# Leaving out the 18 products of zeros with which TensorE begins

## The reference

```
# layer 0: an FFN with low-rank corrections chosen by batch, then 4 rounds of a mixture of experts
h   = relu(x @ wi.T + 2*(x @ ca.T) @ cb.T + 2*(x @ Ea[id].T) @ Eb[id].T)
y   = h @ wo.T + 2*(...common...) + 2*(...expert id of the batch...)
for r in range(4):
    top2 softmax weights cw from y @ Wg[r] + bg[r]          # 4 experts
    y += sum_e cw[e] * (gelu(y @ W1[e] + b1[e]) @ W2[e] + b2[e])
x = x + y
# layer 1: a low-rank map chosen by batch, then a gated FFN
z = (x @ A[lang].T) @ B[lang].T + emb[lang]
g = silu(z @ w1.T * s1) * (z @ w2.T * s2)
g = gelu(g @ h1.T * t1);  g = gelu(g @ h2.T * t2);  x = x + g @ w3.T * s3
```

## Time and profile before

| | us |
|---|---|
| median of 3 runs | 488.02 (486.09 to 488.29) |
| profiled execution | 487.44 |
| its span, first to last instruction | 485.4 |
| TensorE busy | 479.3 (99% of the span) |
| ScalarE, VectorE busy | 393.9, 386.7 |
| GpSimd busy | 119.0 |

### The profile page before, as it was taken

The page is one execution under the profiler, slowest core; times in us unless marked ns, Lnnn a source line. Parts: engine busy times, 40 slices in busy tenths (PEclk is TensorE's granted clock), DMA queues, the critical chain, the costliest instruction groups (busy, mean ns, idle before and its releaser), DMA issues.

```text
span 485.4 us, 7484 instructions
## 1 busy us (share of the span) xinstructions
PE 479.3 (99%) x2276; PEld 397.8 (82%) x2276; DVE 386.7 (80%) x640; ACT 393.9 (81%) x542; POOL 119.0 (25%) x103
## 2 busy tenths in 40 slices
PE   7999999999999999999999999999999999999997
PEld 6998888888888888888888888888888887888886
DVE  4689899989879898988898898989897758644343
ACT  3789988888888888988888888888888888697653
POOL 3896212121212122121212121231313144400000
PEclk9899999999999999999999999999999999999999
DMA  6802612020202102020202021220202000000001
GB/s 172 251 5 86 213 73 88 3 87 0 89 1 86 54 33 87 0 87 0 87 0 87 1 86 55 76 88 0 87 2 87 1 1 1 0 0 1 0 23 68
DMA packets 6954, 26.30 MB, mean 54 GB/s; under 512 B 2194, under 2 KB 2578, under 8 KB 4754
## 3 DMA queue, kind: packets, MB, share of 16 engines
q1 hardware_dynamic: 5810, 21.20, 12.1%
q0 software_dynamic: 528, 3.67, 2.4%
q10 hardware_dynamic: 592, 1.11, 0.8%
HBM read 24.81 MB, written 1.18 MB: 54 GB/s over the span
## 4 chain that ended last, share of the span: by engine, by line
PE 97%; DMA 1%; POOL 1%; ACTq 1%; issue 0%; ACT 0%; DVE 0%
PE bank L491 35%; PE bank L492 34%; PE bank L495 26%; PE bank L577 1%; PE bank L578 1%; DMA stage<-lora_all 1%; PE bank L513 1%; POOL x L249 0%; POOL ffn_lo L403 0%; PE bank L526 0%; ACTq L252 0%; PE bank L510 0%; ACT L878 0%; ACTq L244 0%; DVE x L1249 0%
## 5 line engine op out<-in xcount | busy, mean ns | idle before, releaser
L794 ACT ACTIVATE act_out<-bank,vec 128x512 f32<-128x512 f32 x256 | 165.6, 683 | 41.6 <-PE bank L495 32.5
L1089 DVE TENSOR_TENSOR hid_lo<-act_out,hid_hi 128x1024 fp32r<-128x1024 f32 x128 | 156.3, 1240 | 33.7 <-ACT hid_hi L799 33.6
L799 ACT ACTIVATE hid_hi<-act_out 128x1024 fp32r<-128x1024 f32 x128 | 135.9, 1062 | 8.6 <-PE bank L495 0.9
L455 POOL TENSOR_TENSOR cur<-cur,prod 128x512 f32<-128x512 f32 x48 | 65.0, 1355 | 237.4 <-DVE prod L1100 236.9
L491 PE MATMUL bank<-hid_hi,moe_hi 128*128 128x512 f32 x256 | 99.9, 390 | 0.0
L495 PE MATMUL bank<-hid_hi,moe_lo 128*128 128x512 f32 x256 | 99.7, 390 | 0.0
L491 PE MATMUL bank<-xhi,moe_hi 128*128 128x512 f32 x256 | 99.7, 390 | 0.0
L492 PE MATMUL bank<-hid_lo,moe_hi 128*128 128x512 f32 x256 | 99.7, 389 | 0.0
L492 PE MATMUL bank<-xlo,moe_hi 128*128 128x512 f32 x256 | 99.6, 389 | 0.0
L495 PE MATMUL bank<-xhi,moe_lo 128*128 128x512 f32 x256 | 99.6, 389 | 0.0
L491 PEld LDWEIGHTS bank<-hid_hi,moe_hi 128*128 128x128 f32 x256 | 48.1, 188 | 11.5 <-issue 0.4
(11 more groups left out here) (125 smaller groups left out, 570.3 us busy)
## 6 DMA issues: line engine op xcount, KB each, us to landing
cw_all<-cw_dram SPq DMA_DIRECT2D x16, 1024.0 KB, 4.6
stage<-ffn_w POOLq DMA_DIRECT2D x1, 2304.0 KB, 8.4
cw_all<-moe_w SPq DMA_DIRECT2D x4, 512.0 KB, 9.8
stage<-lora_all SPq DMA_DIRECT2D x6, 160.0 KB, 3.9
x<-x_t POOLq DMA_DIRECT2D x3, 256.0 KB, 5.5
out_t<-x SPq DMA_DIRECT2D x3, 256.0 KB, 2.5
cur<-cond_base ACTq DMA_DIRECT2D x2, 256.0 KB, 3.6
stage<-ffn_w POOLq DMA_DIRECT2D x1, 512.0 KB, 3.9
```

The lines of the kernel that those rows point to most:

```text
L455: pool.tensor_tensor(cur[:, c, :], cur[:, c, :], prod[:, s % 2, :], ALU.add).then_inc(add_done, 1)
L794: act.activation(act_out[:, f // 2, f % 2, :], bank[:, f, :], ACT.Gelu_apprx_tanh, bias=vec[:, V_B1 + e * FC + f:V_B1 + e * FC + f + 1]).t ...
L799: act.activation(hid_hi[:, s % 2, 2 * pr:2 * pr + 2, :], act_out[:, pr, :, :], ACT.Copy)\
L1089: dve.tensor_tensor(hid_lo[:, s % 2, 2 * pr:2 * pr + 2, :], act_out[:, pr, :, :], hid_hi[:, s % 2, 2 * pr:2 * pr + 2, :].bitcast(F32), ALU ...
```

## The change

The constant that says how many products of zeros TensorE computes goes from 18 to 0. The helper `warm` stays and its loop runs zero times; the wait ahead of it stays too, and so does the fill of `blank`.

```diff
@@ -56,7 +56,7 @@
         1), (7, 0), (6, 1), (7, 1))
 MOE_ORDER = (0, 4, 1, 5, 2, 6, 3, 7)
 FFN_PIECES = 3 + 2 * FC
-WARM = 18
+WARM = 0
 RING = 9
 PREP = 3
 PREP_AT = (2, 6, 10)
```

## The result

| | runs | median us | range |
|---|---|---|---|
| before | 20 | 487.43 | 485.84 to 488.94 |
| after | 20 | 488.70 | 487.60 to 489.66 |

The ratio is 1.0033, 95% interval 1.0023 to 1.0042. I had forecast 487.1, a gain of 0.9 us; the sign was wrong. By the 0.5% that the prediction took as its bound it is no change; by the interval it is a loss of 1.3 us. (The forecast started from the median of the first three runs, 488.02, which was 0.6 above that of 20; so the difference is the fairer measure of it than the time.)

The account below looks back on a forecast made before the run. TensorE, busy 479.3 of 485.4 us, bounds the kernel; only its start could change. A start 0.2 us later against 1.43 regained, with GpSimd's possible cap, gave -0.9 us: from 488.02 to 487.1 us, range 486.2 to 487.9.

Parts of the forecast that it names:

- By the two rows the rise falls at 10.6 to 11.3 us: From rises 4.0 and 3.3 us after unbroken work began: clock up before the first long product, with work from 7.30 us.
- C: Rival: before loses no clock in most runs, the profiled one was unlucky; after 0.2 to 0.75 us slower or more; chance 0.1.
- The largest prize, 1.43 us: First long products: the time their stretch at the lower clock level costs before, 0.15 + 1.22 + 0.06 us.
- Rival A: 32-row merges don't bring the clock up; rise at 16.1 to 16.8 us, +0.9 to +1.2 us; chance 0.25.
- the late start: First long product, in rival A: starts at 12.8 us behind slower merges, a price of 0.75 us.
- the stretch at the lower level: Long products in rival A: 3.3 to 4.0 us at the lower level, costing 1.45 to 1.76 us.
- breakpoint: Rival A: a clock rise later than 14.0 us makes the kernel slower.
- the gain of 0 for the 36 passes themselves: Zeros at the start, 6.18 us: nothing waits behind them, gain 0, bounded by a gap of 0.06 us.
- the factor for merges at the lower level: Merges from 7.30 us: 32-row passes taken to last 1.9 times as long; first two merges from 1.13 to 2.15 us.
- merge group 3: Last merges before the long products: from 10.9 to 12.8 us at the lower level, so first long product at 12.8.
- GpSimd as the cap: Fourth batch: GpSimd's result has 0.7 us of slack, 0.2 spent, capping the gain at 0.5 if GpSimd doesn't move.
- B: Rival: the clock rises at 15.35 us as now, whatever stood ahead; +0.6 us, 488.6 us; chance 0.15.

Follow-up runs that it names:

- two with zeros on 32 rows: Changed kernel with 30 or 14 products of zeros on 32 of 128 rows ahead of the first merge: 495.29 us (one run) and 488.18 us (12 runs).
- the fills on 32 rows: Kernel before plus 2 products of zeros behind merge group 1 and 4 ahead of the first long product, all on 32 rows: 487.17 us, ratio 1.0000.
- all three profiles: Profiles of the changed kernel, first look and two unedited repeats: medians 488.70, 488.30 and 488.22 us; spans 486.6, 486.5 and 485.7 us.
- the third profile: Second unedited repeat of the changed kernel: median 488.22 us of 12 runs, ratio 1.0026 to before, span 485.7 us.
- the fills: Kernel before plus full-array products of zeros in TensorE's two gaps: both 486.51 us, first alone 486.16, second alone 486.17 and again 486.21.
- the second profile of before: Unedited control repeat of the kernel before, profiled in an execution that didn't fall: median 487.27 us of 8 runs, ratio 1.0023, span 484.5 us.
- the first fill alone: Kernel before plus 2 full-array products of zeros behind merge group 1: 486.16 us, ratio 0.9985, 2 of 13 fell.

## Why the prediction was wrong

**"By the two rows the rise falls at 10.6 to 11.3 us": this step failed.** It took the merges for work that raises the clock because they leave TensorE no idle time. They don't, or not enough: in five profiles of kernels that reach the merges at the lower level (three of after, two with zeros on 32 rows), the rise came 2.6 to 5.2 us behind the first long product. (Two of the five distances, 2.6 and 2.9, are shorter than the 3.3 us of before, so merges on several row groups at once may count for a little. That stays open.) The trace of before held the warning: TensorE was busy with merges for all of 9.20 to 11.00 us, and at 11.9 the level was gone. (The prediction gives this moment as 11.94; its own working, 0.12 us before 12, is 11.88.) I read that as the fault of the idle time around them; the fills on 32 rows show that closing it with such work is no cure.

**"C: nothing says that it was unlucky."** That two of the first three runs lay above the profiled execution was taken as a sign that it was a usual one. It was usual for half of the executions; the other half don't fall. The largest prize, 1.43 us, was in half of the executions already won, so even a perfect rise would have gained 0.8 us on the mean (1.4 x 36/91 + 2.8 x 9/91).

**Rival A** had the mechanism and its price on the profiled execution: +0.9 to +1.2 us against 1.2 measured. That the sum fits so well is in part luck, for two of its terms missed and offset each other: the late start was priced at 0.75 and measured 0.28, since the loads landed 0.5 us earlier, and the stretch at the lower level was put at 3.3 to 4.0 us and measured 5.2. Its breakpoint, a rise later than 14.0 us, was passed in all three profiles. Against executions of before that don't fall, the difference is 488.52 (37 runs of after) - 486.07 = 2.4 us, and the parts of the three profiles give as much: 0.4 for the start (the ways from GpSimd's first issue of x, 3.85, 4.07 and 3.29, less the 3.30 of before are 0.55, 0.77 and 0, mean 0.44), 0.15 for the first step, and 0.44 x 4.1 = 1.8 for the stretch.

**Right were** the gain of 0 for the 36 passes themselves (the first merge waits for its load in both); the factor for merges at the lower level (0.99 / 0.54 = 1.83 for the 1.9 taken); TensorE without idle time from the first merge on (but for 0.19 us in the third profile); merge group 3 as the piece that sets the first long product if the clock is still down; and no further difference behind 24 us. GpSimd as the cap was never tested by after, but the fills and the second profile of before tested it: with all steps short, no wait of TensorE for GpSimd shows behind the first long product in them, and an execution without a fall is 1.4 us shorter, so the cap of 0.5 us was too careful.

**B**, a rise at a fixed moment, is ruled out as a rule by 17.5, 17.0, 14.9 and 23.2 us. **A rule of the Trainium skill** (page "TensorE: Matmul & The Clock Gate", section "Why this matters for your kernels") says to warm TensorE up with matmuls ahead of a benchmark, or else the lower clock is measured. The runs agree in part. Without the zeros, the first long product met the lower level in all three profiles; with 18, 46 of 91 executions show no fall. But with 9, over at 5.3 us, the time was that of none (488.42), so what counts is the level at the first long product.

## What to carry to other kernels

Work ahead of the first data can be free and still pay, through the clock: ask which level TensorE has when the first critical product starts, and what ran just before; in this kernel only products on all rows clearly counted. Read the level from the step between equal products, and take several executions of the kernel before as the baseline, sorted by mean clock, before pricing a prize that one profile shows. Four products of zeros in the last gap ahead of the critical stretch, on top of the 18 at the start, ended the falls (0 of 24) and gained 0.7 us on the mean. Whether they would do it without the 18, or more at the start would do as well, was not tried.

## What the runs showed of the hardware that I had not expected

- 60 passes on 32 of 128 rows, 12.7 us without a break, left TensorE at the lower level; on 128 rows the level rose after 4.0 us.
- The level of one kernel fell in 45 of 91 executions and not in the others, at a cost of 1.4 us in 36 of them and 2.8 in 9. The moment of a fall was 11.9 us in the profile of before and 13.3 in that of the first fill alone; that of a rise without full-array zeros was 2.6 to 5.2 us behind the first long product.
- The clock column stood at full until the first change of the clock in every profile, and the mean clock goes with it, so a kernel that starts at the lower level looks better there (1.00) than one that rose and fell (0.996).
